# First attention: K projected two batches ahead, scratch rows laid out for reads in runs of 12 KB, first steps reordered

## The reference

```python
x = x + xattn(layernorm(x), ctx, ctx, mask, wq, wk, wv, wo)
#   xq = (layernorm(x) @ wq) -> [b, 16 heads, 112, 16];  xk, xv likewise from ctx (375 rows)
#   attn = softmax(xq @ xk^T / sqrt(16) + mask);  out = (attn @ xv) @ wo
x = x + ffn(layernorm(x), ...)        # 8 experts, top 2, capacity 560
x = x + softmax(x' @ ctx^T) @ ctx     # second attention, x' = layernorm(x)
x = x + moe(layernorm(x), ...)        # 8 experts, top 2
```

## Time and profile before

| | |
|---|---|
| median of 3 runs | 1207.72 us (1204.66 to 1208.1) |
| profiled execution | 1202.43 us, span 1200.3 us |
| mean granted TensorE clock | 0.895 |
| busy: PE, DVE, ACT, POOL | 967.7, 701.0, 527.5, 469.7 us |
| DMA moved | 160.52 MB, mean 134 GB/s |

### The profile page before, as it was taken

One profiled execution on the slowest core, in us unless ns is written; L12 is line 12 of the kernel. 1 busy time (PEld: TensorE's weight loads), 2 busy tenths in 40 slices (PEclk: granted clock), 3 DMA queues, 4 the chain that ended last, 5 costly groups with the idle time before them and its releaser, 6 DMA issues.

```text
span 1200.3 us, 23049 instructions
## 1 busy us (share of the span) xinstructions
PE 967.7 (81%) x8011; PEld 893.4 (74%) x8011; DVE 701.0 (58%) x1994; ACT 527.5 (44%) x1171; POOL 469.7 (39%) x477
## 2 busy tenths in 40 slices
PE   3488898897988944999999937573699999999994
PEld 3477786786777734899999915452599999999994
DVE  3245575475555563666655536777567767677250
ACT  2376686685866743454444312230234323343120
POOL 3112215215223042444443366355354555544322
PEclk8698898897988876999999978885699999999997
DMA  5997787866966406656666566532543444433101
GB/s 138 231 185 151 168 186 149 164 136 157 176 123 122 84 28 177 170 158 163 191 175 166 166 181 194 170 102 80 172 115 96 105 124 120 119 83 83 18 4 19
DMA packets 123300, 160.52 MB, mean 134 GB/s; under 512 B 10400, under 2 KB 113536, under 8 KB 122784
## 3 DMA queue, kind: packets, MB, share of 16 engines
q1 hardware_dynamic: 112816, 140.65, 48.4%
q0 software_dynamic: 10352, 18.15, 6.3%
HBM read 104.94 MB, written 54.87 MB: 133 GB/s over the span
## 4 chain that ended last, share of the span: by engine, by line
PE 46%; DMA 22%; DVE 12%; issue 6%; POOL 6%; SPq 4%; ACT 2%; DVEq 0%; POOLq 0%; ACTq 0%
PE ps L278 36%; DMA KST<-k_scratch 10%; DMA k_scratch<-KHL 5%; SPq L1575 3%; PE ps L392 3%; DMA y_scratch<-YY 3%; DVE HTH L1215 2%; POOL gth L1500 2%; PE ps L384 2%; PE ps L404 2%; DMA X<-in_x 1%; PE ps L616 1%; DVE WL L869 1%; POOL xg_scratch L1405 1%; POOL rs L1385 1%
## 5 line engine op out<-in xcount | busy, mean ns | idle before, releaser
L278 PE MATMUL ps<-XGH,WH 128*128 128x280 f32 (+1 forms) x768 | 225.4, 293 | 16.8 <-DVE XGL L1201 15.0
L278 PE MATMUL ps<-XGL,WH 128*128 128x280 f32 (+1 forms) x768 | 225.4, 293 | 0.0
L278 PE MATMUL ps<-XGH,WL 128*128 128x280 f32 (+1 forms) x768 | 225.0, 293 | 0.0
L1455 POOL TENSOR_TENSOR HTL<-GT,HTH 128x280 fp32r<-128x280 f32 x128 | 127.6, 997 | 245.9 <-DVE HTH L1215 245.9
L1113 DVE CUSTOM_DVE_ANT_0 NS<-ps,negm 112x375 f32<-112x375 f32 x256 | 137.6, 543 | 132.1 <-PE ps L384 124.7
L713 ACT ACTIVATE PP<-NS,MN 112x375 f32<-112x375 f32 x256 | 157.6, 615 | 25.0 <-DVE MN L1113 24.5
L278 PEld LDWEIGHTS ps<-XGH,WH 128*128 128x128 f32 x768 | 150.4, 196 | 19.9 <-DVE XGL L1201 16.7
L278 PE MATMUL ps<-WH,HTH 128*112 128x256 f32 x568 | 161.9, 285 | 0.3 <-POOL HTL L1455 0.3
L278 PE MATMUL ps<-WH,HTL 128*112 128x256 f32 x568 | 159.4, 281 | 0.0
L278 PE MATMUL ps<-WL,HTH 128*112 128x256 f32 x568 | 159.4, 281 | 0.0
L392 PE MATMUL ps<-cst,PP 112*125 112x112 f32 x768 | 141.2, 295 | 20.0 <-ACT PP L713 15.1
(11 more groups left out here) (212 smaller groups left out, 1911.4 us busy)
## 6 DMA issues: line engine op xcount, KB each, us to landing
WG<-in_v SPq DMA_DIRECT2D x48, 512.0 KB
KST<-k_scratch SPq DMA_DIRECT2D x96, 188.0 KB, 6.6
WG<-in_w SPq DMA_DIRECT2D x32, 512.0 KB
k_scratch<-KHL SPq DMA_DIRECT2D x16, 752.0 KB, 4.0
CT<-in_ctx_t SPq DMA_DIRECT2D x32, 375.0 KB, 5.5
xg_scratch<-zero SPq DMA_DIRECT2D x8, 1289.8 KB
CN<-in_ctx_n SPq DMA_DIRECT2D x16, 375.0 KB
QST<-q_scratch SPq DMA_DIRECT2D x48, 112.0 KB, 4.0
```

The lines of the kernel that those rows point to most:

```text
L278: m = e.matmul(out_ap, l, r, start=n == 0, stop=n == len(steps) - 1)
L1455: e.tensor_tensor(HTL[:, f, cols], GT[:, gi % 3, :], HTH[:, f, cols], ALU.subtract).then_inc(hl_pool[layer], 1)
```

## The change

The scratch tensors get a layout in which, for each of the 32 rows (two heads of a pair x 16), the 8 pairs of heads lie next to each other; a stack read then takes 16 rows of 8 x 376 x 4 bytes (12 KB; for Q 8 x 224 x 4, 7 KB) where it took 128 runs of 1504 (896) bytes. The write is four DMAs of 32 partitions each, and its semaphore counts 64 instead of 16.

```diff
-        k_d = nc.dram_tensor("k_scratch", [2, 2, 2 * 128, KP], F32)
-        q_d = nc.dram_tensor("q_scratch", [2, 2, 2 * 128, 2 * S], F32)
+        k_d = nc.dram_tensor("k_scratch", [2, 2 * HD, 2, H // 2, KP], F32)
+        q_d = nc.dram_tensor("q_scratch", [2, 2 * HD, 2, H // 2, 2 * S], F32)
...
+            def spread(scratch, halves, landed):
+                for m in range(4):
+                    e.dma_start(scratch.rearrange("r t (g m) n -> m r (t g) n", m=4)[m],
+                                halves[32 * m:32 * m + 32].bitcast(F32).rearrange("p t g n -> p (t g) n")).then_inc(landed, 16)
...
             def stack(dst, scratch, terms, landed):
                 for up in range(2):
                     for t in range(3):
                         p = 48 * up + 16 * t
-                        rows = scratch[terms[t]].rearrange("(j e d) n -> e d j n", e=2, d=HD)[up]
-                        e.dma_start((dst[p:p + 16, up] if len(dst.shape) == 4 else dst[p:p + 16]).bitcast(F32), rows).then_inc(landed, 16)
+                        rows = dst[p:p + 16, up] if len(dst.shape) == 4 else dst[p:p + 16]
+                        e.dma_start(rows.bitcast(F32).rearrange("p j n -> p (j n)"),
+                                    scratch[HD * up:HD * up + HD, terms[t]].rearrange("d j n -> d (j n)")).then_inc(landed, 16)
```

SP's lists, before the loop and in it:

```diff
+            weights(0)
             context(0)
-            e.dma_start(wst[:, 0, :, :], wk.rearrange("(k p) n -> p k n", p=128)).then_inc(d_wqkv[0], 16)
-            e.dma_start(X[:, 0:2, :], x[0:2].rearrange("b s d -> s b d")).then_inc(d_x0, 16)
+            rows(0, 2, d_x0)
+            weights(1)
             e.dma_start(cst[:], const).then_inc(d_cst, 16)
-            for i, src in enumerate((wq, wv)):
-                e.dma_start(wst[:, i + 1, :, :], src.rearrange("(k p) n -> p k n", p=128)).then_inc(d_wqkv[i + 1], 16)
+            weights(2)
+            context(1)
             e.dma_start(negm[:], mask).then_inc(d_mask, 16)
-            context(1)
+            rows(2, 4, d_x1)
             write_k(0)
             write_q(0)
             stack_k(0)
             stack_q(0)
-            e.dma_start(X[:, 2:B, :], x[2:B].rearrange("b s d -> s b d")).then_inc(d_x1, 16)
+            context(2)
+            write_k(1)
+            stack_k(1)
+            context(3)
...
+            rows(4, B, d_x2)
...
-            context(2)
...
             for b in range(B):
-                if b + 1 < B:
-                    write_k(b + 1)
-                if b + 3 < B:
-                    context(b + 3)
-                if b + 1 < B:
-                    stack_k(b + 1)
-                if b % 2 == 0 and b + 2 < B:
-                    write_q(b // 2 + 1)
+                if b + 4 < B:
+                    context(b + 4)
+                if b + 2 < B:
+                    write_k(b + 2)
+                    if b % 2 == 0:
+                        write_q(b // 2 + 1)
+                    stack_k(b + 2)
+                    if b % 2 == 0:
+                        stack_q(b // 2 + 1)
...
-                if b % 2 == 0 and b + 2 < B:
-                    stack_q(b // 2 + 1)
```

More of the change, by code:

```diff
@@ L414, in pe_attention0 @@
                 project_v(0, c)
+            for g in range(2):
+                project_k(1, g)
             for b, h in batch_order():
@@ L435, in pe_attention0 @@
                         project_out(b - 1)
-                    if h == 12:
+                    if h == 13:
                         route_x(b - 1)
[L438 to L441, removed]
+                if 2 <= b < B + 2:
+                    if h == 1:
+                        route_logits(b - 2)
+                    if h == 11 and ends_chunk(b - 2) is not None:
+                        route_counts(ends_chunk(b - 2))
         def pe_flags(e, layer):
@@ L729, in act_attention0 @@
             context_hi(1)
+            for g in range(2):
+                k_hi(1, g)
             for b, h in batch_order():
@@ L1073, in dve_attention0, with weights_lo, context_lo @@
         def dve_attention0(e):
[L1074 to L1077, removed]
+            def weights_lo(i):
+                hi, lo = ((wkh, wkl), (wqh, wql), (wvh, wvl))[i]
                 e.wait_ge(w_hi, i + 1)
                 e.tensor_tensor(lo[:], wst[:, i, :, :], hi[:], ALU.subtract).then_inc(w_lo, 1)
+            def context_lo(b):
+                e.wait_ge(ch_done, b + 1)
+                e.tensor_tensor(CL[:], CT[:, b % 2, :, :], CH[:], ALU.subtract).then_inc(cl_done, 1)
             def stats1(b):
@@ L1139, in x_added @@
                 dve_stats(e, 2 + b % 2, b, var2)
+            weights_lo(0)
+            context_lo(0)
             for b in range(2):
                 stats1(b)
+            weights_lo(1)
+            for b in range(2):
+                dve_normed(e, b, b, rs1, b + 1, xn1)
+            weights_lo(2)
             for g in range(2):
@@ L1146, in dve_attention0 @@
                 x_lo(b)
+            q_lo(0)
+            e.memset(ps[:, 5, :], 1.0).then_inc(pvo_done, 1)
             e.wait_ge(d_mask, 16)
             e.tensor_scalar(negm[:], negm[:], -1.0, None, ALU.mult).then_inc(negm_done, 1)
-            q_lo(0)
+            context_lo(1)
+            for g in range(2):
+                k_lo(1, g)
             routes = []
@@ L1154, in dve_attention0 @@
                     head_min(n - 1)
-                if b % 2 and b + 1 < B and h == 0:
+                if b % 2 and b + 1 < B and h == 1:
                     q_lo(b // 2 + 1)
@@ L1415, in context_lo @@
                 e.tensor_tensor(CL[:], CT[:, b % 2, :, :], CH[:], ALU.subtract).then_inc(cl_done, 1)
-            context_lo(0)
             for b in range(2):
                 pool_rsqrt(e, b, b + 1, var1, rs1)
-                pool_normed(e, b, b, rs1, xn1)
+            for p in range(2):
+                e.memset(QST[:, p].bitcast(F32), 0.0).then_inc(stack_z, 1)
             e.memset(VV[:, :, :, :, HD:2 * HD], 1.0).then_inc(setup, 1)
@@ L1439, in pool_attention0 @@
                     pool_normed(e, 2 + (b - 1) % 2, b - 1, rs2, xn2)
-                if b >= 3 and h == 0 and ends_chunk(b - 3) is not None:
+                if b >= 3 and h == 6 and ends_chunk(b - 3) is not None:
                     pool_scatter(e, 0, ends_chunk(b - 3))
```

107 lines of the change are left out of this document (56 added, 51 removed).

## The result

The changed kernel took 1198.86 us (1187.91 to 1206.53) against 1203.65 (1198.55 to 1208.31) for the kernel before in runs beside it, a ratio of 0.9945 (95% interval 0.9921 to 0.9968): 4.8 us faster by the medians and 6.6 by the ratio, not 37. Its profiled execution took 1198.55 us with a span of 1196.6; the mean granted clock is 0.900 (0.895 before).

What follows compares the result with a forecast made beforehand. It took writing K's halves to DRAM and reading them back as stacked rows (15% of the span) as the bound; start -12, loop -18.6, batch 14 and tail -6.5 made -37, so 1171 us, range 1147 to 1196.

Steps and rivals of the forecast that it cites:

- Start, up to K's projection: Kernel start: wk asked for first, context cast next, its low half on DVE; projection at about 7.3, 5.1 us earlier.
- QST is zeroed on POOL instead ... so it is hidden: Kernel start: POOL's zero fills, 3.2 us per half, done by about 17; SP needs QST past 20, so no cost.
- Q's chain: Loop: from an odd batch's first scores, Q's halves written and read back as stacks, landing after 21.6 us (20 to 26).
- the trace agrees with the first (129): Stack reads to 16 partitions: the trace's 129 GB/s was said to match the skill's 104 GB/s for partitions 0 to 15.
- the lateness: Loop: odd batches of 20.2 us leave Q 1.4 us late, six times, costing 8.4 us (0 to 35).
- Waits of 1.25 left the clock up: Loop: PE's short waits, such as those on late Q, were taken not to lower PE's granted clock.
- -8 for the clock: Batches 2 to 13: less running at 1.2 GHz once the waits go saves 8 us (0 to 13).
- Q in time: Rival: Q's reads get faster by long runs or writes overlap fully, so no waits; 1154 us, chance 0.25.
- my case: Main forecast: 1171 us for the kernel, 1160 to 1182 by its bounds, chance 0.45.
- On POOL the scatter ... 2 us each, 4: Batches 6 and 10: the scatter delays the context's low half, PE waits in step 12; 4 us together (0 to 8).
- Batch 14 and the tail, -6.5: Batch 14 without K's projection falls from 27.7 to about 21 us, -6.7; later last routes add 0.2.

Runs made afterwards that it cites:

- zero_later: Changed kernel with one added wait: POOL zeroes QST only after DVE has made the low half of wv; 0.9910 of the kernel before, 1192.28 us.
- after_again: The changed kernel, unedited, run again in the fourth set (no standstills); 0.9852 of the kernel before, 1174.86 us.
- scatter_tail: Changed kernel with the scatters of batches 6, 10 and 14 issued behind the last batch; 0.9924 of the kernel before.
- scatter_step0: Changed kernel with only POOL's scatter put back from step 6 to step 0, third set (no standstills); 0.9872 of the kernel before.
- before_again: The kernel before, unedited, run again for its trace in the fourth set (no standstills); ratio 1.0017.
- before_spread: Kernel before with its scatters' eight indirect DMAs issued one by one in steps 1, 3, ... 15 instead of all in step 0; 0.9948.
- old_layout_again: Changed kernel with the old scratch layout, one write each, run again in the fourth set (no standstills); 0.9739 of the kernel before.
- the second and the third set: Groups of follow-up runs beside the kernel before: the second has standstills, the third none; the kernel before took 1203.7 to 1204.8 us with standstills, 1190.0 and 1191.9 without.

## Why the prediction was wrong

- **Start, up to K's projection: right.** It began at 6.72 (7.3 said); the context's low half on DVE took 0.94 (0.95).
- **"QST is zeroed on POOL instead ... so it is hidden": the first step that failed.** The fills' length was right (6.12 for 6.4), their effect was not: they held DVE's second normalisation for 7.1 us. The step that was wrong is the overlap: POOL was idle, but what it did stopped DVE. With that alone mended (zero_later) every later figure of the start comes out: stack reads at 19.11 (19.1 said), batch 1 at 54.5 (55), batch 2 at 83.3 (81.5); only the first scores, at 34.9 for 36.7, came earlier.
- **Q's chain: right.** From batch 3's first scores at 116.59 to batch 4's at 138.36 it is 21.8 (21.6 said; by the landings of Q for batches 4 to 14 the mean is 21.5). The prediction's "the trace agrees with the first (129)" was generous, as 129 is a quarter above the 104 beside it. Odd batches without their successor's wait took 19.8 to 21.9, mean 20.6 (20.2), and the lateness was 6.5 us over six batches (8.4 said).
- **"Waits of 1.25 left the clock up", and -8 for the clock: failed.** The windows behind batch 4's start, in the changed kernel (wait of 1.95 us) and in after_again (1.73):

```profile
138.40:146.00 7.60, 7.60 (x70) 6.24 (x71) 3.76 (x14) 3.88 (x9) 3.42 (x6) 0.55 0.76 262
```
```profile
139.70:147.00 7.30, 7.15 (x89) 5.97 (x90) 5.21 (x19) 4.92 (x13) 3.95 (x6) 1.00 0.73 258
```

  The granted clock of 0.55, nearly all at 1.2 GHz, made batch 4 23.6 us where it is 21.0 at full clock. Being late by little cost 2.5 us on top, at batches 4 and 12. The length of the wait does not decide it: in the first 7.6 us, batch 4 had 1.00 behind a wait of 2.25 us in scatter_tail and 0.58 behind one of 1.52 in scatter_step0, and in after_again batch 8 had 0.50 behind 1.92. Before, where K's passes stood in steps 1 and 3, the same stretch behind a wait of 4.65 had 0.76; that their going made it worse is argued, not tested. Over the loop the clock hardly rose with standstills (0.90 before), and rose without. The changed kernel; then before_again and after_again:

```profile
60.00:410.00 350.00, 304.51 (x3018) 258.87 (x3017) 202.68 (x730) 250.84 (x602) 98.76 (x115) 0.91 0.79 161
```
```profile
60.00:410.00 350.00, 304.10 (x3064) 265.06 (x3064) 205.84 (x735) 254.06 (x611) 101.26 (x116) 0.89 0.76 154
60.00:410.00 350.00, 305.02 (x3173) 260.16 (x3171) 212.18 (x767) 259.80 (x626) 100.82 (x118) 0.95 0.79 163
```

  Even there the 8 us are not in the time: the ten batches from 2 to 13 that hold no scatter, waits on stacks left out, took 212.4 us where they had taken 210.8 (217.8 and 209.4 with standstills). The lateness itself came from the layout: the rival "Q in time" had 1154, 17 us under my case, and the old layout took 13 off.
- **"On POOL the scatter ... 2 us each, 4": failed.** It named the right instruction and the wrong price. Without standstills the wait for the low half is 4.4 us each and batches 6 and 10 take 27.8 and 27.4 against 21.0 for batch 4: 13 us by one trace. With them the three scatters hold PE's signals, and so ACT and DVE, for 20 us of chain, and spreading them is worth 13 us (0.9945 to 0.9836). Without standstills spreading was not run by itself. The sign was in the trace of before, and I left it unpriced: in batch 10 the transposes ended at 287.69, and ACT's copy of them started 3.3 us later, as in batches 6 and 14:

```profile
286.72 0.97 PE L392 MATMUL ps<-cst,PP 112*125 112x112 f32 x3
```
```profile
290.95 0.45 ACT L719 ACTIVATE PT<-ps 125x336 f32<-125x336 f32 x1 [9.62 <-PE ps L392]
```

  That the rest of the standstill lay inside the wait on K there is argued from the 6 us of before_spread.
- **Batch 14 and the tail, -6.5:** without standstills batch 14 went from 23.75 to 17.84; with them its scatter took all of it back (27.7 to 27.8).

The sum, by the two traces, of the 33 us that did not come: the start is 10, of which zero_later gives 8.4 to the fills. The scatter is 11.5: batches 6 and 10, without the wait at their ends, took 8.7 longer than before where 4 was said, and batch 14 took 6.8 more than the 21 of the forecast. The clock is 13: the 8 not won, and batches 2, 4, 8 and 12, also without the wait at their ends, together 4.8 longer than before. The odd batches and Q's lateness came out 3 better than said, the tail 2 worse. This is one trace against one, and that it adds up is no proof of each. By timings the scatter is less: spreading it is worth 13 us in the changed kernel, but 6 in the kernel before, so some 7 of its cost is new, against the 4 said; the two do not agree, and how the miss divides between scatter and clock stays open.

The chains of K and Q did what was forecast; the fills, the clock and the scatter took the gain. What makes the standstill stays open. scatter_tail shows that it goes with the scatter, and the semaphores show that it is PE that is waited for: with standstills PE's updates come up to 8.4 us after the modelled ends while the eight DMAs are issued (batch 14 of the changed kernel), and 3.2 us in batch 10 of the kernel before; in the loops of before_again, after_again and old_layout_again none of the heads' updates comes over 1.5 us late. No run shows why. The expectations put it down to the chip, but the second and the third set, one of each kind, carry the same chip number in the record.

## What to carry to other kernels

When a wait is removed, look for what was hidden in it: here a standstill that cost half as much (6 us against 13) while PE was waiting anyway. A step moved to an idle engine is free only if that engine does not share something with the one that is busy. And a layout for longer runs must be priced with the write that it needs: here it gained nothing on the reads and cost 13 us, by the issues of the split writes and by reads that landed a little later.

## What the runs showed of the hardware

- DVE's normalisation (two columns of scalars, SBUF to SBUF, 0.41 us alone) waited through three fills of POOL in a row and took 7.48 us. The Trainium skill, "SBUF — State Buffer", section "Who interferes with whom", says that a tensor_scalar can take the pair of ports that DVE shares with GpSimd, and that whichever of the two issues first then holds the pair for its whole instruction while the other is blocked. The trace agrees, and the wait went over three instructions.
- Four DMAs of 188 KB took SP 2.5 us to issue, 6.0 at worst (at 84.07 in the changed kernel), where one of 752 KB took 0.38.
- While POOL issued eight indirect DMAs of 112 rows, 1.25 us apart, PE's semaphore updates came late in the four sets with standstills, in batch 10 of the changed kernel by up to 7.9 us, with those of 285.7 to 287.9 all arriving between 293.2 and 294.9; ACT and DVE stood from 3.4 us after the first issue to 1.7 after the last. In the two other sets it was not so.
- Two batch starts behind waits of 1.95 and 1.73 us went on at a granted clock of 0.55 and 1.00.
